# Where the query and key rows of unit 1 are loaded, in a fused attention kernel on one core

## The reference

```
q, k, v = x @ Wq.T, x @ Wk.T, x @ Wv.T                # 16 heads of 32
scores  = q k^T / sqrt(32), -inf where mask            # one 512x512 mask for all
out     = softmax(scores) v, all heads side by side, @ Wo.T
x       = x + rmsnorm(out) * rms_scale * (1 + scale(cond)) + shift(cond)
x       = x + quaternion_rotation(fft filter(x))       # constant gate: a 512-wide linear map per token
```

## Time and profile before

| what | value |
|---|---|
| median of 3 runs | 865.63 us (865.63 to 866.34) |
| profiled execution, its own time | 866.87 us |
| span of the profiled execution, first to last instruction | 865.1 us |
| PE busy | 850.7 us (98% of the span) |
| DVE, ACT, POOL busy | 629.5, 616.0, 482.6 us |
| mean granted PE clock | 0.995 of full speed |
| chain that ended last, PE's share | 94% |
| batch 7 of the projection | from about 237 to 270 us of the span |

### The profile page before, as it was taken

The page is one execution under the profiler, slowest core; times in us unless marked ns, Lnnn a source line. Parts: engine busy times, 40 slices in busy tenths (PEclk is TensorE's granted clock), DMA queues, the critical chain, the costliest instruction groups (busy, mean ns, idle before and its releaser), DMA issues.

```text
span 865.1 us, 17179 instructions
## 1 busy us (share of the span) xinstructions
PE 850.7 (98%) x5344; PEld 642.7 (74%) x5344; DVE 629.5 (73%) x1524; ACT 616.0 (71%) x1504; POOL 482.6 (56%) x346
## 2 busy tenths in 40 slices
PE   9999999999979999999999999999999999999997
PEld 6788888888867767776777767777677767777774
DVE  4521321322327889999899998999999998999886
ACT  6232332332317889999999999999999999999882
POOL 0999990000000112477577766777667775777794
PEclk9999999999998999999999999999999999999999
DMA  8954644644695667687766777578767778669201
GB/s 285 343 204 167 224 170 182 230 178 174 207 282 197 146 145 192 151 210 158 180 174 149 161 180 195 124 183 210 164 152 179 163 161 196 157 146 235 84 25 50
DMA packets 82355, 153.76 MB, mean 178 GB/s; under 512 B 8520, under 2 KB 9160, under 8 KB 82272
## 3 DMA queue, kind: packets, MB, share of 16 engines
q1 hardware_dynamic: 82128, 152.49, 65.0%
q10 hardware_dynamic: 144, 0.26, 0.1%
HBM read 102.35 MB, written 50.36 MB: 177 GB/s over the span
## 4 chain that ended last, share of the span: by engine, by line
PE 94%; DMA 1%; DVE 1%; SPq 1%; issue 1%; ACT 1%; POOL 0%; DVEq 0%; ACTq 0%
PE banks L788 26%; PE banks L120 14%; PE banks L816 13%; PE banks L851 10%; PE banks L471 9%; PE banks L472 9%; PE banks L473 9%; PE banks L797 2%; DMA q_scratch<-late 1%; PE banks L831 1%; PE banks L456 1%; PE banks L444 1%; SPq L90 0%; SPq L86 0%; DVE probs L685 0%
## 5 line engine op out<-in xcount | busy, mean ns | idle before, releaser
L137 ACT ACTIVATE probs<-probs,least 128x512 f32<-128x512 f32 x512 | 363.3, 713 | 0.1
L129 DVE CUSTOM_DVE_ANT_0 probs<-banks,mask_bias 128x512 f32<-128x512 f32 x512 | 330.4, 683 | 37.6 <-PE banks L120 37.6
L788 PE MATMUL banks<-ident,probs 128*128 128x128 f32 x2048 | 306.4, 272 | 0.7 <-DVE turned_probs L901 0.6
L788 PEld LDWEIGHTS banks<-ident,probs 128*128 128x128 f32 x2048 | 252.3, 140 | 56.8 <-ACT probs L137 1.8
L120 PE MATMUL banks<-k_rows,q_rows 128*128 128x512 f32 x496 | 237.4, 481 | 5.6 <-DVE least L129 5.6
L901 DVE COPY turned_probs<-banks 128x512 f32<-128x512 f32 x256 | 175.8, 687 | 2.3 <-PE banks L788 2.3
L400 DVE SCALAR_TENSOR_TENSOR late<-banks,late 128x512 fp32r<-128x512 f32 x64 | 43.9, 690 | 167.0 <-ACT late L337 166.8
L1013 ACT ACTIVATE turned_probs<-banks 128x512 f32<-128x512 f32 x256 | 147.1, 587 | 16.9 <-PE banks L788 13.6
L337 ACT ACTIVATE late<-banks 128x512 fp32r<-128x512 f32 x64 | 38.2, 598 | 128.1 <-PE banks L473 112.3
L685 POOL TENSOR_TENSOR late<-rot,late 128x2048 f32<-128x2048 f32 x28 | 129.3, 4619 | 0.0
L816 PE MATMUL banks<-turned_probs,v_sb 128*32 128x512 f32 (+1 forms) x1088 | 116.9, 570 | 1.3 <-ACT turned_probs L1013 1.3
(11 more groups left out here) (134 smaller groups left out, 1269.3 us busy)
## 6 DMA issues: line engine op xcount, KB each, us to landing
q_rows<-q_scratch SPq DMA_DIRECT2D x128, 256.0 KB, 6.0
k_rows<-k_scratch SPq DMA_DIRECT2D x124, 256.0 KB, 6.6
q_scratch<-late SPq DMA_DIRECT2D x64, 256.0 KB, 2.4
k_scratch<-late SPq DMA_DIRECT2D x64, 256.0 KB, 2.3
v_sb<-v_scratch SPq DMA_DIRECT2D x8, 1024.0 KB, 11.6
out<-late SPq DMA_DIRECT2D x29, 256.0 KB, 7.3
raw<-in_xT SPq DMA_DIRECT2D x7, 1024.0 KB, 5.6
v_scratch<-v_out SPq DMA_DIRECT2D x28, 256.0 KB, 2.0
```

The source lines that it names most:

```text
L129: dve.tensor_tensor_reduce(self.probs[:, n % RING, :], self.ps[:, n % SCORE_BANKS, :], self.mask_bias[:, c, :], 1.0, 3e38, ALU.add, ALU.mi ...
L137: act.activation(self.probs[:, n % RING, :], self.probs[:, n % RING, :], ACT.Exp, bias=self.least[:, n % 32:n % 32 + 1], scale=-1.0, accum ...
L788: last = pe.transpose(turn_bank("tile", n)[:, j * P:(j + 1) * P], probs[:, n % RING, j * P:(j + 1) * P], ident[:, :])
```

## The change

The eight loads of unit 1 leave the head of batch 7. Each Q and K load now follows a pair of K stores of batch 7, as the loads of unit 0 did and do in batch 6. The loads themselves, their sizes and the semaphores that they raise stay as they were, and no wait is added in the source.

```diff
             def batch(b, p, more, unit=None):
-                for c in range(TC):
-                    if unit != 1:
-                        store_v(b, c)
-                    else:
-                        rows.load_q(sp, 1, c)
-                        rows.load_k(sp, 1, c)
+                for c in range(TC) if unit != 1 else ():
+                    store_v(b, c)
...
                     for g in range(NG):
                         store_qk(b, which, g)
-                        if unit == 0 and which == 1:
-                            rows.load_q(sp, 0, g)
-                            rows.load_k(sp, 0, g)
+                        if unit is not None and which == 1:
+                            rows.load_q(sp, unit, g)
+                            rows.load_k(sp, unit, g)
```

## The result

| | before | changed kernel |
|---|---|---|
| median of 6 runs each, same chip | 865.87 us (865.52 to 867.43) | 860.9 us (860.24 to 862.87) |
| ratio | | 0.9945, 95% interval 0.9931 to 0.9959 |
| span of the profiled execution | 865.1 us | 858.8 us |
| its own time | 866.87 us | 860.58 us |

The change makes the kernel faster, by 5.0 us or 0.55%. I had forecast 857.6 and a range up to 859.9. The direction is right, and so are the wait that goes and the place of the one that comes; the size of the new wait is not. The time lies 1.0 us outside the range and 3.3 above the forecast.

What follows compares the result with a forecast made beforehand. PE, busy 98% of the span, was taken as the bound. Span 865.1 - 9.06 (pause and slow clock) + 1.0 (new wait) = 857.0; median 865.63 - 8.06 = 857.6 us, range 856.2 to 859.9.

Steps and rivals of the forecast that it cites:

- The pause behind m = 5: In batch 7 PE stands before score tile 3 as a Q store lands late; removing this, with the slow clock, gains 9.06 us.
- The split of the 9.06 us: PE's loss around score tile 3 in batch 7: 5.73 us of pause and 3.33 us of the same work at lower clock.
- The wait at score 16: Unit 1's rows, now loaded last, come late for score tile 16; PE waits there 1.0 us.
- the lower bound: Last row load of unit 1 lands after 4.1 us, at 267.4, in time for score tile 16 by 0.3 us.
- Less a tenth: The queue estimate of 1.1 us lateness at score tile 16 was reduced to 1.0 us of waiting.
- The clock behind that wait: PE keeps its full clock behind the wait at score tile 16, as after a 0.82 us pause; nothing added.
- The estimate of 859.5: With 189 GB/s for 32-partition transfers, a queue step takes 4.06 us, unit 1's last row lands at 270.6, sum 859.5.
- 1.24 us: The profiled execution of the kernel before lay this far over the median of its runs, 866.87 against 865.63.
- The second: Rival, chance 0.13: rows clearly later at score tile 16, 2.1 us late for 858.7, up to 3 us for 859.6.
- first: Rival, chance 0.22: rows come in time for score tile 16, all of the 9.06 us stays, 856.6.
- third: Rival, chance 0.04: nothing gained, unit 0's loads alone hold batch 7's Q stores up, landing near 257; 865.6.
- fourth: Rival, chance 0.05: slower than before, PE stops at score tile 16 from 5.8 us on and the clock falls; 867.4.

Runs made afterwards that it cites:

- the second and third experiment: Changed kernel with the 1 MB values load behind unit 1's last row load: 857.53 us; changed kernel with unit 1's row loads behind batch 7's Q stores: 857.23 us.
- both moves: Changed kernel with unit 1's row loads behind the Q stores and the values load behind the last K store: 857.9 us, ratio 0.9907.
- half of the change: Changed kernel with two pairs of unit 1's row loads left at the head of batch 7, two behind the last K-store pairs: 859.48 us, ratio 0.9922.
- the last experiment: Changed kernel with all eight row loads of unit 1 in one burst behind batch 7's last K store: 867.31 us, ratio 1.0011.

## Why the prediction came out as it did

**The pause behind m = 5: right.** It was the burst of row loads in front of the Q stores. The store landed at 247.7 as worked out, and the kernels that have next to no wait at either place lie 8.7 and 9.0 us under the kernel before (the second and third experiment), or 8.0 (both moves), for a forecast 9.06. Half of the burst gave nearly half of the store's delay, 4.4 of 9.6 us. ACT had no wait for a store in batch 7, the clock stayed at 1.00 in every stretch of 1 us from 250 on, and the first transpose came at 260.32, as I had said that the profile would show.

**The split of the 9.06 us: a part misnamed.** I put 3.33 us down to the lower clock. By the experiment with half of the burst the three scores behind the wait are spaced by DVE's masks at full clock too. In the kernel before they run from 259.34 until the next matmul at 261.16 in the same rhythm, 0.61 us each:

```profile
261.16 0.63 PE L471 MATMUL banks<-o_hi,w_hi_k 128*128 128x512 f32 x1
```

So some 1.1 of the 3.33 us were masks and 2.2 the clock. The sum is not touched.

**The wait at score 16: right place, wrong size.** This is the step that failed: "It starts from the 1 MB of values ... then 1 MB at 409 GB/s, 2.56 us, until 254.4". The load took until 256.4, 4.5 us behind the Q store in front of it and not 2.56. I had priced it with a rate from a full queue, and here it is issued 2 us before that store lands. The seven kernels with the load in one piece fall into two groups:

| kernel | values issued | transfer in front lands | values land | between |
|---|---|---|---|---|
| before | 250.0 | 261.2 | 263.6 | 2.4 us |
| rows behind the Q stores | 250.8 | 258.6 | 260.8 | 2.2 us |
| half of the change | 249.6 | 256.0 | 258.5 | 2.5 us |
| values behind the rows | 263.7 | 267.7 | 272.2 | 4.5 us |
| both moves | 262.8 | 264.8 | 268.9 | 4.1 us |
| changed kernel | 249.9 | 251.9 | 256.4 | 4.5 us |
| all rows at the end | 250.4 | 252.4 | 257.0 | 4.6 us |

Issued 6 us or more before the transfer in front lands, the load adds 2.2 to 2.5 us; issued 2 to 4 us before, it adds 4.1 to 4.6. Why is not shown. That the queue had run dry can't be all of it: behind the rows it had not (389 and 387 GB/s from 268 to 270), though row loads of unit 2 were issued beside it there.

With a row that I had not drawn on, part of it could have been seen: the 1 MB loads of x take 5.6 us to land in the median on the page of the profile, which gives 255.6 for a load issued at 250.0, 0.8 short of what came. The experiments with the values moved and halved show that this load alone makes the rows late. The steps of 3.60 us behind it were right (14.2 us for four), and the lower bound nearly so (267.7 landed where the values were gone, 267.4 forecast). "Less a tenth" had no ground. The wait of 2.98 us came just under the 3 us from which I had called myself wrong.

**The clock behind that wait: wrong for its true length.** I added nothing, from a row with 0.82 us of idle time. At 1 us this may well hold: with 0.76 to 0.83 us idle none of the ten executions of two kernels was under 0.999. At 2.6 to 2.8 us it doesn't: by their mean clocks half of the 14 executions lost it, for 1.6 us in the two that a profile shows.

**Transfers into 32 partitions.** For the transfers into 32 partitions, "SBUF — State Buffer" in the Trainium skill, section "Door 1: The DMA port swizzle", had 189 GB/s at 1 MiB beside a limit of about 218. The estimate of 859.5 from that page came out nearer than mine, but not for its reason: in the last experiment the first K load lands at 268.0 and the last at 275.3, and six loads in 7.3 us are 1.22 each, or 215 GB/s, so the trace agrees with the limit and not with the lower figure.

**The balance.** In the spans the sum closes. I had 857.0; the pause is 1.98 us longer (2.98 instead of 1.0) and the first transpose 0.11 us earlier than forecast, which gives 858.9, and 858.8 was measured. The second failed step is the one from the span to the median. With the pause of 2.98 alone my sum would give 859.6, inside the range. But I took off 1.24 us because the profiled execution of the kernel before lay so far over the median of three runs. Against the medians of larger samples (865.87 to 866.24) it lies over by 0.6 to 1.0, and the changed kernel's profiled execution (860.58) lies 0.3 under its median. Those 0.3 are the clock: two of the six executions are at 0.997, and the other four have a median of 860.58. So the 3.3 us are 1.8 in the span, 1.2 taken off and 0.3 for the clock.

**The rivals.** The second had the right place and size (rows up to 3 us late, 859.6) and lacked the clock; the first, third and fourth did not happen. In the third is a slip without effect: 257 lies 10.6 us behind the last load of unit 0 at 246.4, and not 9.7.

## What to carry to other kernels

A burst of loads put in front of stores that an engine soon waits for delays those stores by the whole burst's queue time; what the engine loses is that less what it had to spare. Where it can be spread over steps that leave the queue time to drain, ahead of the need and behind the urgent stores (here a pair behind each Q store), it costs nothing: 857.2 us (ratio 0.990 to the kernel before) against 860.9 (0.9945). A transfer that does not hurry, like the values, does not belong in front of one that does. Where little is queued ahead of it, its price is to be read from a load of the same size in that position. When a pause is forecast, price the clock behind it for the upper bound of its length too, and not from a row with a much shorter one.

## What the runs showed of the hardware that I had not expected

The same kernel with the same idle time of 2.6 to 2.8 us (in the five profiles) kept PE's clock at 2.4 GHz in seven executions and lost it in seven, by their mean clocks, for 1.6 us in the two where a profile shows it. After 2.3 us of idle time it was kept in five of five (mean clock 0.999). In a pause of 7.1 us it fell before PE went on, and the ten executions of that kernel have 0.993 to 0.996. And a load of 1 MB that landed 2.2 to 2.5 us behind the transfer in front of it in a queue that was full landed 4.1 to 4.6 us behind it when it was issued only 2 to 4 us before; in the changed kernel the DMA engines moved 186 to 238 GB/s in its first 3 us.
